# Vision tower on one core: twelve images instead of six in the buffer that feeds the masked value copies, and the first expert weights on the scalar engine's queue

## The reference

```python
h = _L0_tok_ref(x, ...)                                   # patches, W, two layernorms, positions
h = concatenate([broadcast_to(cls_tok, ...), h], axis=1)  # 38 tokens an image
h = h + _L0_attn_ref(_layernorm(h), w_attn, w_proj)       # causal, 16 heads of 16, quantised weights
h = h + _L0_ffn_ref(_layernorm(h), weight, aux1, aux2, bias)   # tanh(h W A1 A2 + b)
h = h + _L1_attn_ref(_layernorm(h), Wq, bq, ..., head_mask)
h = h + _L1_ffn_ref(_layernorm(h), Wg, bg, W1, b1, W2, b2)     # 16 experts, 76 slots each
```

## Time and profile before

| what | value |
|---|---|
| median of three runs | 445.86 us (443.11 to 446.62) |
| the profiled execution | 444.86 us, of which its span 443.2 us |
| PE busy | 370.4 us, 84% of the span |
| DVE, POOL, ACT busy | 235.5, 178.0 and 113.7 us |
| mean granted TensorE clock | 0.892 |

### The profile page before, as it was taken

The page is one execution under the profiler, slowest core; times in us unless marked ns, Lnnn a source line. Parts: engine busy times, 40 slices in busy tenths (PEclk is TensorE's granted clock), DMA queues, the critical chain, the costliest instruction groups (busy, mean ns, idle before and its releaser), DMA issues.

```text
span 443.2 us, 9050 instructions
## 1 busy us (share of the span) xinstructions
PE 370.4 (84%) x3164; PEld 307.6 (69%) x3164; DVE 235.5 (53%) x675; ACT 113.7 (26%) x333; POOL 178.0 (40%) x264
## 2 busy tenths in 40 slices
PE   4649998799998989887858667984499999999992
PEld 3537886687787968766747546764398888888881
DVE  1298998687887368565666474465022232222221
ACT  0001233344444445343423322211021101111010
POOL 0224566665556537344536451645011313132221
PEclk9968999899999989888997895555589999999998
DMA  8997011110122212223233323531868999999200
GB/s 296 401 429 299 23 42 33 35 46 30 34 82 91 60 55 84 87 73 88 75 105 85 112 76 103 138 124 32 211 214 275 317 317 324 315 315 324 66 16 5
DMA packets 39237, 64.68 MB, mean 146 GB/s; under 512 B 5147, under 2 KB 30684, under 8 KB 38368
## 3 DMA queue, kind: packets, MB, share of 16 engines
q1 hardware_dynamic: 32752, 53.86, 36.7%
q10 hardware_dynamic: 2208, 6.82, 4.4%
q0 software_dynamic: 4240, 3.51, 3.0%
HBM read 53.20 MB, written 7.62 MB: 137 GB/s over the span
## 4 chain that ended last, share of the span: by engine, by line
PE 59%; issue 12%; DMA 8%; DVE 7%; SPq 6%; POOL 5%; ACT 1%; ACTq 1%; DVEq 0%; POOLq 0%
PE bank L919 13%; PE bank L932 12%; SPq L599 6%; PE bank L782 5%; PE bank L806 5%; PE bank L867 4%; DMA early<-in_xt 4%; PE bank L853 4%; PE bank L816 3%; DMA v<-vt 3%; PE bank L842 3%; PE bank L834 2%; PE bank L874 2%; POOL mid L662 2%; PE bank L791 1%
## 5 line engine op out<-in xcount | busy, mean ns | idle before, releaser
L675 POOL TENSOR_TENSOR mid<-v,tab 114x512 f32<-114x512 f32 x32 | 34.4, 1078 | 74.8 <-DMA v<-vt 51.9
L919 PEld LDWEIGHTS bank<-mid,early 128*128 128x128 f32 x512 | 61.9, 199 | 1.2
L919 PE MATMUL bank<-mid,early 128*128 (+1 forms) x512 | 61.9, 281 | 0.0
L932 PE MATMUL bank<-early,mid 128*76 128x256 f32 x256 | 57.9, 379 | 0.0
L853 PE MATMUL bank<-mid 114*38 114x51 f32 (+3 forms) x768 | 31.7, 232 | 21.2 <-issue 18.8
L853 PEld LDWEIGHTS bank<-mid 114*38 114x38 f32 (+1 forms) x768 | 28.8, 141 | 27.3 <-issue 25.2
L932 PEld LDWEIGHTS bank<-early,mid 128*76 128x76 f32 x256 | 36.6, 147 | 15.4
L712 POOL DMA_DIRECT2D mid<-in_b x14 | 7.9, 563 | 84.0 <-DVE idx L1228 84.0
L662 POOL TENSOR_TENSOR mid<-mid,tab 128x608 f32<-128x608 f32 x32 | 38.5, 1209 | 1.9 <-PE bank L834 1.8
L655 POOL TENSOR_TENSOR rs<-rs,mhalf 114x1 f32<-114x1 f32 (+4 forms) x60 | 36.8, 613 | 5.0
L806 PE MATMUL bank<-xnT,attn 128*128 128x228 f32 (+1 forms) x192 | 38.4, 355 | 0.0
(11 more groups left out here) (112 smaller groups left out, 588.9 us busy)
## 6 DMA issues: line engine op xcount, KB each, us to landing
early<-in_w SPq DMA_DIRECT2D x64, 512.0 KB, 5.1
v<-vt SPq DMA_DIRECT2D x192, 38.0 KB
expert_in<-k_empty SPq DMA_DIRECT2D x1, 2570.0 KB, 37.0
attn<-in_attn SPq DMA_DIRECT2D x2, 1024.0 KB, 19.5
early<-in_xt ACTq DMA_DIRECT2D x1, 1536.0 KB, 35.9
early<-in_xf SPq DMA_DIRECT2D x1, 1368.0 KB, 20.1
mid<-expert_in SPq DMA_DIRECT2D x8, 160.6 KB, 6.6
mid<-expert_in ACTq DMA_DIRECT2D x8, 160.6 KB, 7.0
```

Source lines behind the costliest of these rows:

```text
L675: eng.tensor_tensor(Vb[0:TROWS, (m - 1) % 3, :, :, 0:HD], v3[:, at:at + 2, :].rearrange("p a (h d) -> p a h d", h=HEADS), bc(bc(blockm[:, ...
L919: ins = mm(Hp[b][:, c // 4, (c % 4) * ECOLS:(c % 4 + 1) * ECOLS], w1s[s][:, kc, c * 128:c * 128 + 128], xeT[:, bass.ds(it * SLOTS + s, 1), ...
L932: ins = mm(Yp[b][0:CAP, 0:DIM], hT[:, b, c, :], w2s[s][:, c, :], start=c == 0, stop=c == HC - 1)
```

## The change

- `v3` becomes two halves of six images: `v3a`, a tile of its own, and `v3b`, which lies over the tanh block's input matrices in `early` (`temp_`). An image's place is its number through both layers modulo 12 (`VIMGS`). The third tile's copies wait for `fW`, the step that last reads those matrices.
- SP's wait before a tile's copies is now for the `vb` of the images 12 places back, and there is none before the first four tiles.
- POOL's `vb` waits for the copies of the tiles that its own two images lie in; before, it always waited for the tile of its later image and for the tile ahead of that one.
- The 16 first weight loads leave SP. They are steps `w` of ACT in the planner, issued from ACT's queue (L563 and L568 of the changed kernel), the first after a wait for `tok` 10. The loads of the later experts stay on SP.
- The planner's tables get other numbers: all of `GOAL`, `LAYER`, `EAGER`, SP's price and handover. So the orders of all engines differ.

```diff
+VIMGS = 12
-PAIR, TILE, LAYER, EAGER = 7.41, 13.22, 126.9, 529.73
+PAIR, TILE, LAYER, EAGER = 7.41, 13.26, 122.3, 311.95
...
-        "sp": {"v": 5.4, "tok": 0.1}}
-HANDOVER = {"pe": 0.22, "dve": 0.1, "act": 0.12, "pool": 0.12, "sp": 2.0}
+        "sp": {"v": 5.6}}
+HANDOVER = {"pe": 0.22, "dve": 0.1, "act": 0.12, "pool": 0.12, "sp": 3.0}
...
-            spread = l * PAIRS + ((TILE_IMGS * (t - 1) - 1) // 2 + 1 if t >= 2 else 0)
-            step("sp", "v", l, t, ("act", "v", l, t), *pair("pool", "vb", spread - 1))
+            images = 2 * PAIRS * l + TILE_IMGS * t + rows(t) // SEQ
+            step("sp", "v", l, t, ("act", "v", l, t), *pair("pool", "vb", (images - 1 - VIMGS) // 2), *([("act", "fW", 0, 0)] if m == 2 else []))
...
-    step("sp", "tok", 0, TILES - 1, ("dve", "tok", 0, TILES - 1))
+    for m in range(4 * SLOTS):
+        step("act", "w", 0, m, ("dve", "tok", 0, TILES - 1))
...
-        v3 = sb("v3", [TROWS, 2 * TILE_IMGS, DIM])
+        v3a = sb("v3a", [TROWS, 6, DIM])
+        v3b = temp_[0:TROWS, 0:6 * DIM].rearrange("p (a n) -> p a n", a=6)
...
             for kind, l, n in order("sp"):
-                if kind == "tok" and n == TILES - 1:
-                    emptied(sp, uses[(kind, l, n)])
-                    slots_free = True
-                elif kind == "v":
-                    m = l * TILES + n + 1
-                    emptied(sp, uses[(kind, l, n)])
-                    pairs = l * PAIRS + ((TILE_IMGS * (n - 1) - 1) // 2 + 1 if n >= 2 else 0)
-                    if pairs:
-                        sp.wait_ge(vb_ready, pairs)
-                    for a in range(rows(n) // SEQ):
-                        for j in range(3):
-                            sp.dma_start(v3[...], vt[...]).then_inc(v_spread[(m - 1) % 2], 16)
-                    if slots_free and first_loads:
-                        load, s, half = first_loads.pop(0)
-                        load(s, slice(s, s + 1), half)
-            for load, s, half in first_loads:
-                load(s, slice(s, s + 1), half)
+                m = l * TILES + n + 1
+                first = 2 * PAIRS * l + TILE_IMGS * n
+                count = rows(n) // SEQ
+                emptied(sp, uses[(kind, l, n)])
+                if m == 3:
+                    emptied(sp, uses[("fW", 0, 0)])
+                if first + count > VIMGS:
+                    sp.wait_ge(vb_ready, (first + count - 1 - VIMGS) // 2 + 1)
+                for a in range(count):
+                    for j in range(3):
+                        sp.dma_start(v3(first + a, 1)[...], vt[...]).then_inc(v_spread[(m - 1) % 2], 16)
...
-                    for u in (t - 1, t):
-                        if u >= 0:
-                            pool.wait_ge(v_spread[u % 2], v_spread_count(u))
+                    for u in sorted({l * TILES + image // TILE_IMGS for image in (2 * n, 2 * n + 1)}):
+                        pool.wait_ge(v_spread[u % 2], v_spread_count(u))
...
+                elif kind == "w":
+                    if n == 0:
+                        emptied(act, uses[("tok", 0, TILES - 1)])
+                    load, s, half = first_loads[n]
+                    load(act, s, slice(s, s + 1), half)
```

More of the change, by code:

```diff
@@ L169, in bc @@
     return v.to_broadcast(shape)
-PAIR, TILE, LAYER, EAGER = 7.41, 13.22, 126.9, 529.73
-GOAL = {"xs": -80.1, "cs": -215.9, "bs": -113.4, "asum": -20.1, "qs": -171.8, "fB": -118.7, "fW": 6.3, "wo": 51.3, "bo": 9.8,
[3 rows of a table removed]
+PAIR, TILE, LAYER, EAGER = 7.41, 13.26, 122.3, 311.95
+GOAL = {"xs": -93.1, "cs": -310.0, "bs": -102.8, "asum": 15.0, "qs": -223.3, "fB": -96.3, "fW": 10.1, "wo": 45.6, "bo": -63.5,
[3 rows of a table added]
 COST = {"pe": {"cs": 3.5, "bs": 2.6, "qs": 0.3, "fB": 1.75, "fW": 1.75, "bo": 0.9, "tok": 2.62, "lnt": 0.36, "qk": 3.12, "v": 0.88, "s0": 0.85, "s1": 0.62,
@@ L183 @@
         "pool": {"xs": 0.95, "tok": 0.9, "lns": 0.9, "km": 1.33, "vb": 1.12, "lnx": 0.78, "cnt": 0.36, "scat": 1.3},
-        "act": {"fB": 0.65, "fW": 0.65, "lnt": 0.4, "qk0": 1.15, "qk1": 1.9, "v": 0.42, "s": 0.74, "pt": 0.72, "ot": 0.5, "ffn": 0.45, "log": 0.55},
-        "sp": {"v": 5.4, "tok": 0.1}}
-HANDOVER = {"pe": 0.22, "dve": 0.1, "act": 0.12, "pool": 0.12, "sp": 2.0}
+        "act": {"fB": 0.65, "fW": 0.65, "lnt": 0.4, "qk0": 1.15, "qk1": 1.9, "v": 0.42, "s": 0.74, "pt": 0.72, "ot": 0.5, "ffn": 0.45, "log": 0.55, "w": 0.55},
+        "sp": {"v": 5.6}}
+HANDOVER = {"pe": 0.22, "dve": 0.1, "act": 0.12, "pool": 0.12, "sp": 3.0}
 ARRIVES = {("pe", "cs"): 6.0, ("pe", "bs"): 6.0, ("dve", "asum"): 10.0, ("dve", "wo"): 25.0, ("pe", "fB"): 22.0}
@@ L270, in needs @@
             step("act", "pt", l, p, ("pe", "pt", l, p), *pair("pe", "pv", m - 2))
-            step("pool", "vb", l, p, *[("sp", "v", l, u) for u in (t - 1, t) if u >= 0], *pair("pe", "pv", m - 3))
+            step("pool", "vb", l, p, *[("sp", "v", l, u) for u in (2 * p // TILE_IMGS, t)], *pair("pe", "pv", m - 3))
             step("pe", "pv", l, p, ("act", "pt", l, p), ("pool", "vb", l, p), *pair("dve", "pv", m - 1))
@@ L282, in wanted @@
         return GOAL[kind]
+    if kind == "w":
+        return GOAL[kind] + 8 * n
     if kind == "xs":
@@ L540, in v_spread_count, with v3 @@
             return sum(16 * 3 * (rows(v % TILES) // SEQ) for v in range(u % 2, u + 1, 2))
+        def v3(image, count):
+            at = image % VIMGS
+            half = v3a if at < 6 else v3b
+            return half[:, at % 6:at % 6 + count, :]
         def g_use(n):
@@ L548, in emptied, with half_w1, half_w2 @@
             eng.wait_ge(g_free[b], g + 1)
+        def half_w1(queue, s, e, half):
+            queue.dma_start(w1s[s][:, half, :], i["in_w1"][e, half * 128:(half + 1) * 128, :].rearrange("e p n -> p (e n)")).then_inc(w1_here[s], 16)
+        def half_w2(queue, s, e, half):
+            at = slice(half * HC // 2, (half + 1) * HC // 2)
+            queue.dma_start(w2s[s][:, at, :], i["in_w2"][e, half * HID // 2:(half + 1) * HID // 2, :].rearrange("e (c p) n -> p (e c) n", p=128)).then_inc(w2_here[s], 16)
+        first_loads = [(load, s, half) for s in range(SLOTS) for load in (half_w1, half_w2) for half in range(2)]
         out_rows = out.rearrange("b s n -> (b s) n")
@@ L571, in _ @@
             sp.dma_start(xbuf.rearrange("(p r) n -> p (r n)", p=128), k["k_empty"]).then_inc(l_zero, 16)
[L573 to L580, removed]
@@ L582, in _ @@
-            first_loads = [(load, s, half) for s in range(SLOTS) for load in (half_w1, half_w2) for half in range(2)]
-            slots_free = False
-            for kind, l, n in order("sp"):
-                if kind == "tok" and n == TILES - 1:
-                    emptied(sp, uses[(kind, l, n)])
-                    slots_free = True
-                elif kind == "v":
-                    m = l * TILES + n + 1
-                    emptied(sp, uses[(kind, l, n)])
-                    pairs = l * PAIRS + ((TILE_IMGS * (n - 1) - 1) // 2 + 1 if n >= 2 else 0)
-                    if pairs:
-                        sp.wait_ge(vb_ready, pairs)
-                    for a in range(rows(n) // SEQ):
-                        for j in range(3):
-                            sp.dma_start(v3[j * SEQ:(j + 1) * SEQ, (TILE_IMGS * n + a) % (2 * TILE_IMGS), :], vt[a * SEQ:(a + 1) * SEQ, (m - 1) % 2, :]).then_inc(v_spread[(m - 1) % 2], 16)
-                    if slots_free and first_loads:
-                        load, s, half = first_loads.pop(0)
-                        load(s, slice(s, s + 1), half)
@@ L604, in _ @@
-            for load, s, half in first_loads:
-                load(s, slice(s, s + 1), half)
+            for kind, l, n in order("sp"):
+                m = l * TILES + n + 1
[8 more added lines that the diff above has]
+                    for j in range(3):
+                        sp.dma_start(v3(first + a, 1)[j * SEQ:(j + 1) * SEQ, 0, :], vt[a * SEQ:(a + 1) * SEQ, (m - 1) % 2, :]).then_inc(v_spread[(m - 1) % 2], 16)
@@ L617, in _ @@
                     for half in range(2):
-                        half_w1(s, bass.ds(it * SLOTS + s, 1), half)
+                        half_w1(sp, s, bass.ds(it * SLOTS + s, 1), half)
                     sp.wait_ge(y_full[s % 2], it * (SLOTS // 2) + s // 2 - 1)
                     for half in range(2):
-                        half_w2(s, bass.ds(it * SLOTS + s, 1), half)
+                        half_w2(sp, s, bass.ds(it * SLOTS + s, 1), half)
         @block.gpsimd
@@ L665, in _ @@
                     m = l * PAIRS + n + 1
-                    t = l * TILES + (2 * n + 1) // TILE_IMGS
-                    for u in (t - 1, t):
-                        if u >= 0:
-                            pool.wait_ge(v_spread[u % 2], v_spread_count(u))
+                    for u in sorted({l * TILES + image // TILE_IMGS for image in (2 * n, 2 * n + 1)}):
+                        pool.wait_ge(v_spread[u % 2], v_spread_count(u))
                     if m > 3:
                         pool.wait_ge(o_full, m - 3)
```

(3 more changed lines are left out.)

## The result

The changed kernel takes 432.98 us (median of four runs, 431.02 to 436.08) against 444.75, a ratio of 0.975 (95% interval 0.971 to 0.979). It is faster by 2.5%, where 6% was forecast; 433 us is the time that the second rival, the burst, was given. The profiled execution took 431.02 us.

What follows compares the result with a forecast made beforehand. Layer 1 was taken as bound by SP's copies and POOL's masked copy waiting for each other over a six-image buffer. The sum 444.86 - 27.5 - 3 + 3 = 417.4 us was given as 418 us, range 404 to 436.

Steps and rivals of the forecast that it cites:

- the second rival, the burst: Layer 0, tiles 0.7 to 0.9: the loads' burst starves the copies, some 18 us lost, 433 us; chance 0.14.
- the term for the sixteen loads: Layer 0: issue on ACT and DMA contention of the 16 weight loads cost 3 us, bounds 0 and 8.
- the slower rival: Layer 0: ACT stands still while it issues, 5.1 us a load, delaying it 52 us, 470 us; chance 0.06.
- Twelve images: Layer 1: with twelve images the turn no longer bounds, a gain of 27.5 us of 122, bounds 21.6 and 35.7.
- thin margins (b): Layer 1: values need 12.5 us to masked copy, PE has 11.6 to 16.1 us of steps; a few waits stay.
- Layer 0 without the loads: Layer 0: copy waits are behind some of 8.7 us of idle PE; 3 us gained, bounds 0 and 6.
- Tail and experts: After layer 1: a faster clock might give up to 3 us in the tail, none taken; experts 0.
- Layer 0's pace: Layer 1 gets layer 0's 6.7 us a pair and no better, a gain of 14.8 us, 431 us; chance 0.16.
- no earlier start: Value copies start no earlier, so more room is of no use, and the time stays at 445 us; chance 0.07.

Runs made afterwards that it cites:

- run 2: The changed kernel with each of the 16 first weight loads cut to 64 KB, an eighth, issues and places kept; 417.2 us, ratio 0.937.
- paced loads: Loads on ACT, eight behind single steps late in layer 0, eight near the attention's end: changed kernel 425.6 us (0.956); old orders with twelve images 415.8 us (0.936).
- run 11: Old orders, twelve images, loads on ACT, first eight from pair 0.14's exponent on, the others about the end of layer 1; 413.4 us, ratio 0.931.
- run 7: Old tables and orders, twelve images, loads on ACT, eight from pair 0.13's exponent on, the others near the attention's end; 415.8 us, ratio 0.936.
- run 1: The changed kernel with its 16 first weight loads back on SP, one behind each tile's copies from tile 0.7 on; 430.5 us, ratio 0.968.
- run 3: The kernel before with only the twelve-image buffer: old tables and orders, loads on SP; 425.9 us, ratio 0.951.
- late loads: First eight loads on ACT placed later in layer 0, the others near the attention's end: changed kernel 420.6 us (0.946); old orders with twelve images 413.4 us (0.931).
- run 4: The kernel before, six-image buffer and old orders, with only the 16 loads moved to ACT at the changed kernel's places; 449.5 us, ratio 1.010.
- run 8: The changed kernel with all sixteen loads in the tail, from pair 1.14's pt on; 426.1 us, ratio 0.959.
- run 9: Old tables and orders, twelve images, the sixteen loads on ACT in a burst at the changed kernel's places; 431.4 us, ratio 0.973.
- run 5: The changed kernel, burst kept, with the 38-row copies of tiles 0.7 to 0.9 cut into 32 and 6 rows; 424.0 us, ratio 0.955.

## Why the prediction was wrong

**The step that failed is the term for the sixteen loads.** I took 3 us for issue and contention together, bounds 0 and 8. With the same orders and the bytes gone the time is 417.2 for 433.0 (run 2): the term is 15.8 us. The old orders with the burst and with paced loads give 431.4 - 415.8 = 15.6, or 18.0 against run 11. With the six-image buffer layer 0 lost 17.8. Without the term the rest of the sum comes near: 27.5 + 3 = 30.5 us were forecast, and with small loads the span is 27.2 shorter, 3.7 to masked copy 0.15, 23.4 from there to 1.15 and 0.1 behind it. That 417.4 and 417.2 agree so closely is luck, since one has 3 us for the loads in it and the other next to none.

I had the pieces: 26.6 us of DMA work, tiles 0.7 to 0.9 beside it, two of sixteen engines for the copies by their share of 0.14, and 18 us as the price of the rival. I went wrong in three places. I took the loads to spread over "some 40 us"; eleven of them went out within 14 us, since ACT's program has room between its compute steps, and the DMA engines stood at 0.99 for 15 us and not at 0.6. I then gave the measured speed of issuing at the program's start as evidence against harm; it was evidence only against the slower rival. And I weighed the likeliest case by its bounds, though the rival's own count gave 18 us.

**Twelve images: right, inside its bounds.** SP no longer waits for a masked copy (75.4 us before). From 0.15 to 1.15 the gain is 27.3 us, and 27.5 was forecast. That it fits so well is luck in part: without the burst the same orders gain 23.4 (run 2, where the granted clock from 172 to 260 us was 0.86), and the old orders 27.1 (run 7), in bounds of 21.6 to 35.7. In layer 1's 92 us PE is busy for 82.96 at a clock of 0.93, 77.2 us of full-clock work, or 0.84 of the time for my 0.85. A pair takes 5.6 us, inside 5.5 to 6.2. PE's wait before pv there fell under 5 us, POOL's before the masked copy to 17.7, over the 15 that I named:

```profile
POOL mid L673 <- DMA v3a<-vt: 10.2, 3, 4.9
...
POOL mid L673 <- DMA early<-vt: 7.5, 3, 3.7
...
PE bank L851 <- issue: 4.5, 4, 2.5
```

These are the thin margins (b), five waits of 1.8 to 4.9 us. But the buffer could give this only because the loads left layer 1. With the loads among its copies on SP, layer 1 from 1.0 to 1.15 takes 98.0 us in the new orders (run 1) for 84.2 (changed kernel) and 87.4 (run 2), and 99.7 in the old (run 3) for 83.0 (run 7). I had put the loads in the queue down as 0.43 us of issue. They cost 11 to 17 us of layer 1, and 10 to 13 us of the whole time (430.5 - 417.2, 425.9 - 415.8 or 413.4), less than the burst's 16 to 18. So moving them into the burst lost time: a ratio of 0.951 with the loads on SP and 0.973 with the burst, both with twelve images and old orders. No run has the loads in layer 1 on ACT's queue, so whether the shared queue cost the 11 to 17 us, or only the meeting of loads and copies, stays open.

**Layer 0 without the loads: right.** I took back 3 us there. With small loads 0.15 starts at 163.44 for 167.17, 3.7 us earlier (run 2); in the old orders the buffer alone brought it to 160.62 (run 3), 6.6 earlier and a little past my bound of 6.

**New tables: worth nothing, or less.** I gave them no term. With the burst both orders are equal (0.975 and 0.973). Without it the old orders are faster in all three pairs: 0.951 and 0.968 with the loads on SP, 0.936 and 0.956 with paced loads, 0.931 and 0.946 with late loads, with intervals apart. The paced and late loads meet other copies in one order than in the other, so only the pair on SP compares the orders alone.

**Tail and experts: right.** 1.7 us were gained from 1.15 to the end, in a bound of 0 to 3.

**The rivals.** The burst came, near the price and at the time that it was given, at 14%. It is not shared evenly by three tiles as I had reckoned: 10.8 of the 18.9 us at masked copy 0.15 are there at 0.10. Layer 0's pace and no earlier start did not come. ACT standing still: not as it was put, since eleven issues took 14 us and not the 56 of 5.1 us each, but single issues did hold it for 4 to 6 us, which the start of the program had not shown.

## What to carry to other kernels

Find a turn in which each of two queues waits for the other, and add up its pieces: a buffer twice as deep then gives what the stretch's own work allows, here 23 to 27 us once the weight loads were out of the stretch. Before moving bulk transfers out of a latency-bound queue, look at when they will run and not only at who issues them: the same 8 MB cost 10 to 13 us among layer 1's copies, and in a burst 16 to 18 us, both against loads of an eighth the size or loads kept mostly in the gaps. Price the burst for the small transfers by themselves; here copies of 38 rows, divided into 32 and 6, gave back 9 us of it. And when several things are changed at once, take the change apart: the buffer with the old orders and loads in the gaps was worth 6.9%, the whole change 2.5%.

## What was not expected of the hardware

- An issue can hold its engine. Ten transfers in a row at the program's start took 0.43 to 0.93 us each, and loads of 64 KB never over 0.8 us. In the bursts of 512 KB loads the ninth took 4.1 to 6.0 us on ACT (runs 4, 8 and 9, and the changed kernel, where it is most of the 4.72 for two). But in run 5, with the same loads before it, the ninth and tenth took 1.42 us together. What limit it meets, no run shows.
- Beside full DMA engines SP needed 8.66 and 11.83 us to issue nine copies of 38 rows, and 11.78 for eighteen of 32 and 6 rows.
- How much of the burst's 16 us is ACT held at its issues stays open in part. The first 10.8 us, at masked copy 0.10, are the copies' own delay. Behind it, tile 0.8's copies begin 2.5 us later than with small loads, and by that start ACT's long issue can't account for more. Dividing the copies gave back 9.0 us of the time, and ACT's long issue was gone with it, so that run doesn't part the two.
